# A two-layer attention and expert kernel: first loads in pieces, key reload issued from two queues, last round reordered

## What is computed

```
x = x + attention1(norm(x), ctx)          # 16 heads of 8, softmax over all 1601 context rows
x = x + experts1(norm(x))                 # 9 experts of 352, two chosen per token, sigmoid gate
x = x + attention2(norm(x), ctx, idx)     # 64 context rows per token, named by idx (all below 256)
x = x + experts2(norm(x))                 # 8 experts of 176, two chosen, softmax gate, and a shared one
experts:  sum_e  cw[t, e] * (silu(x w1[e]) * (x w3[e])) w2[e]
attention2: the rows in idx count as often as they are named (a count per token and context row)
```

## Time and profile before

| | us |
|---|---|
| median of 3 runs | 1551.48 (1540.69 to 1551.87) |
| the profiled execution's own time | 1554.78 |
| its span | 1553.0 |
| PE busy | 1381.9 |
| DVE busy | 1105.1 |

### The profile page before, as it was taken

The page is one execution under the profiler, slowest core; times in us unless marked ns, Lnnn a source line. Parts: engine busy times, 40 slices in busy tenths (PEclk is TensorE's granted clock), DMA queues, the critical chain, the costliest instruction groups (busy, mean ns, idle before and its releaser), DMA issues.

```text
span 1553.0 us, 34000 instructions
## 1 busy us (share of the span) xinstructions
PE 1381.9 (89%) x12530; PEld 805.4 (52%) x12588; DVE 1105.1 (71%) x2284; ACT 776.7 (50%) x1191; POOL 825.1 (53%) x1379
## 2 busy tenths in 40 slices
PE   4499899999998899989988999989999899889966
PEld 3143474347743476435843476435754467335835
DVE  4586468877688567986598767886688776895353
ACT  3155525762376524764266723765257633665242
POOL 4146345664457445665457554675456744553542
PEclk9698899999999999999999999999999999999977
DMA  3704330023201431024300331013200231002201
GB/s 87 164 12 127 80 78 1 22 75 85 55 8 30 85 75 41 12 50 94 82 1 32 66 92 46 12 40 104 66 18 22 68 80 42 2 2 57 56 1 45
DMA packets 97622, 82.12 MB, mean 53 GB/s; under 512 B 17626, under 2 KB 90612, under 8 KB 97460
## 3 DMA queue, kind: packets, MB, share of 16 engines
q1 hardware_dynamic: 97460, 79.95, 20.9%
HBM read 67.29 MB, written 12.61 MB: 51 GB/s over the span
## 4 chain that ended last, share of the span: by engine, by line
PE 61%; DVE 20%; issue 6%; POOL 6%; ACT 4%; DMA 2%; SPq 1%; POOLq 0%; DVEq 0%; ACTq 0%
PE ob L763 11%; PE ob L837 8%; DVE mx L1216 7%; PE um L821 7%; PE um L822 6%; PE um L748 6%; PE um L733 5%; PE um L711 3%; DVE big L1327 2%; DVE mx L1331 2%; DVE xn L1115 2%; PE um L883 2%; DVE big L1260 2%; PE um L686 1%; PE um L705 1%
## 5 line engine op out<-in xcount | busy, mean ns | idle before, releaser
L1216 DVE TENSOR_REDUCE mx<-um 128x2 f32<-128x802 f32 (+1 forms) x512 | 501.0, 988 | 173.5 <-PE um L733 169.9
L1021 ACT ACTIVATE probs<-um 128x1024 f32<-128x1024 f32 (+1 forms) x448 | 425.7, 962 | 210.2 <-PE um L748 205.7
L1406 POOL TENSOR_TENSOR hid<-hid,cwb 128x256 f32<-128x256 f32 (+1 forms) x304 | 216.9, 730 | 279.2 <-DVE hid L1228 134.6
L1027 ACT ACTIVATE hid<-um 128x256 f32<-128x256 f32 (+1 forms) x304 | 116.8, 384 | 357.2 <-PE um L822 357.1
L1412 POOL TENSOR_TENSOR big<-iotab,idx_lo 128x512 bf16<-128x512 bf16 x256 | 272.5, 1079 | 30.8 <-PE um L923 23.0
L763 PE MATMUL ob<-probs,vaug 128*9 128x256 f32 (+1 forms) x3328 | 280.6, 386 | 2.6 <-ACT oT L1003 2.0
L733 PE MATMUL um<-kst,qa 64*128 64x401 bf16 (+1 forms) x1024 | 178.4, 347 | 29.7 <-DVE mx L1216 16.6
L748 PE MATMUL um<-big,kst 64*128 64x256 bf16 (+1 forms) x1664 | 171.0, 279 | 10.1 <-DVE mx L1216 3.9
L1228 DVE TENSOR_TENSOR hid<-hid,um 128x256 f32<-128x256 f32 (+1 forms) x304 | 124.7, 415 | 67.3 <-ACT hid L1027 64.6
L821 PE MATMUL um<-xnT,w1T 128*128 128x256 f32 (+1 forms) x400 | 128.0, 402 | 0.0
L837 PE MATMUL ob<-w2T,hid 128*128 128x128 f32 (+1 forms) x800 | 123.6, 279 | 3.5 <-POOL hid L1406 2.5
(11 more groups left out here) (218 smaller groups left out, 2065.4 us busy)
## 6 DMA issues: line engine op xcount, KB each, us to landing
kst<-k_parts SPq DMA_DIRECT2D x384, 50.0 KB
cwb<-cw_rows SPq DMA_DIRECT2D x112, 128.0 KB, 3.5
k_parts<-big SPq DMA_DIRECT2D x72, 128.0 KB, 1.9
ctx_sb<-in_ctx SPq DMA_DIRECT2D x8, 768.0 KB
cwb<-cw_rows SPq DMA_DIRECT2D x48, 96.0 KB, 3.0
k1st<-k_parts SPq DMA_DIRECT2D x96, 32.0 KB
cwb<-cw_rows SPq DMA_DIRECT2D x48, 64.0 KB, 2.7
cwb<-cw_rows SPq DMA_DIRECT2D x16, 112.0 KB, 3.1
```

The lines of the kernel that those rows point to most:

```text
L1021: act.activation(probs[0:kn, k:k + 2, 0:w], own_banks, ACT.Exp).then_inc(f_read, 1)
L1216: dve.tensor_reduce(mx[:, p % 2, s, :, j], pair[:, :, 0:w], AX, ALU.max, negate=True).then_inc(u_read, 1)
L1406: pool.tensor_tensor(h, h, cwb[0:nr, k, :], ALU.mult).then_inc(hw_ready, 1)
```

## The change

Loads: the context of batch 0 comes in four pieces with a semaphore each (`ctx0_in`), with `Wkv` and the key bias between them (`wkv_in`), then `x`; `Wo`, `bv`, `Wq`, `bqs`, `bo` (`wa_in`, now five) and the indices last; the gate bias goes with the square weights. PE waits for one piece per `ctx`, and for `wa_in` in a new event `pre`, at -46.9. ACT first copies two values (its table load comes with it). The memset of `kst` is split between POOL (pairs 0, 1) and DVE, that of `k1st` goes to POOL behind `idx`. Reload of batch 0: SP issues the half `hh = 0`, ACT the other. `x`, indices and context of batch 1 are issued at -31.95, between `rel` 0 and `rel` 1. `all0` of batch 0 stands behind `ctx` 3. Expert weights are transposed from 23.127 on (before 14.886), `w2T` from 42.939 (45.331).

Last round: the pairs of batch 6's attention 2 start at `XL - 6.339 = 49.66` of round 7, 3.0 apart; its layer norm and gate chain 24.258 before `XL`'s place (so `nm1` at 78.94, `ct1` at 88.13); its layer-2 chunks at `R + 0.422`, 0.489 apart, in front of and among the lone attention 2 of batch 7. The reload of `k1st` is an event `rel1` of its own; for batch 7 it comes at 81.33, `kv1` at 85.56 and `mq` at 86.08. Layer-1 chunks of batch 7 no longer wait in the order for layer 2 of batch 6. `SHIFT` moves 19 named events by 0.02 to 0.73 units in all batches.

```diff
-'pairl': 1.461, 'c1': 6.259, 'b_all0': -41.0, 'b_w1': 14.886, 'b_w2': 45.331, 'b_w2s': 1.6
+'pairl': 1.336, 'c1': 6.247, 'b_all0': -37.556, 'b_w1': 23.127, 'b_w2': 42.939, 'b_w2s': 1.387
+'b_pre': -46.9, 'b_ldc1': -31.95, 'z_rel1': 25.333, 'z_kv1': 29.559, 'z_mq': 30.079, 'z_pair0': -6.339, 'z_pair': 3.0, 'z_back': -24.258, 'z_chunk': 0.422, 'z_each': 0.489
+SHIFT = {('cnt', 11): -0.621, ('part', 44): 0.293, ('mu', 2): -0.526, ('eq', 14): 0.727, ('c0', 6): 0.325, ...}
-                at.append((t, len(at), kind, b, n))
+                at.append((t + SHIFT.get((kind, n), 0.0), len(at), kind, b, n))
-                put(prep + AT["ldx"], "ldx", b)
-                put(prep + AT["ldc"], "ldc", b)
+                put(prep + AT["ldx"] if b >= 2 else AT["b_ldc1"], "ldx", b)
+                put(prep + AT["ldc"] if b >= 2 else AT["b_ldc1"], "ldc", b)
...
+                put(own + (AT["kk1"] + 0.01 if b < NB - 1 else XL + AT["z_rel1"]), "rel1", b)
+                put(own + (AT["kv1"] if b < NB - 1 else XL + AT["z_kv1"]), "kv1", b)
...
+                first, back, chunk, each = chain + AT["pair0"], chain, chain + Y1, C1
+                if b == NB - 2:
+                    step, first, back = AT["z_pair"], chain + XL + AT["z_pair0"], chain + XL + AT["z_back"]
+                    chunk, each = chain + R + AT["z_chunk"], AT["z_each"]
...
-            sp.dma_start(wkv_sb[:, :], Wkv).then_inc(wa_in, 16)
+            load_ctx0(0)
+            sp.dma_start(wkv_sb[:, :], Wkv).then_inc(wkv_in, 16)
+            load_ctx0(1)
+            sp.dma_start(bk_col[:, :], bkv[0:D].rearrange("(p a) -> p a", a=1)).then_inc(wkv_in, 16)
+            load_ctx0(2)
+            sp.dma_start(xs[0][:, :, :], x[0:1].rearrange("a (s p) d -> p (a s) d", p=P)).then_inc(x_in, 16)
+            load_ctx0(3)
...
-                        for hh in range(2):
+                        for hh in range(1 if b == 0 else 2):
                             r = SLOT * hh + HD * term
                             sp.dma_start(kst[r:r + HD, 2 * n:2 * n + 2, 0:NK], src[hh, :, 2 * n:2 * n + 2, :]).then_inc(kst_in[n], 16)
...
+                elif kind == "rel" and b == 0:
+                    if n == 0:
+                        act.wait_ge(key0_out, 16 * 3 * 4)
...
+                    for term in range(NT):
+                        src = k_parts[0, KPART[term]].rearrange("(a h d) k -> h d a k", h=2, d=HD)
+                        r = SLOT + HD * term
+                        act.dma_start(kst[r:r + HD, 2 * n:2 * n + 2, 0:NK], src[1, :, 2 * n:2 * n + 2, :]).then_inc(kst_in[n], 16)
...
+            copy(veps[:, :, :], neg_half[:, :, :]).then_inc(act_warm, 1)
...
+            dve.memset(kst[:, 2:NP, :].rearrange("p a k -> p (a k)").bitcast(f32), TWO_ONES).then_inc(kst_half, 1)
...
+            pool.memset(kst[:, 0:2, :].rearrange("p a k -> p (a k)").bitcast(f32), TWO_ONES).then_inc(kst_one, 1)
```

More of the change, by code:

```diff
@@ L67, in rows @@
+SHIFT = {('cnt', 11): -0.621, ('part', 44): 0.293, ('part', 45): 0.198, ('part', 26): -0.337, ('cnt', 14): -0.483, ('df', 28): -0.156, ('df', 7): 0.309, ('df', 8): 0.309, ('w1', 1): -0.211, ('pair1', 7): 0.319, ('part', 3): -0.1, ('part', 57): -0.306, ('key', 3): -0.019, ('cnt', 12): -0.118, ('mu', 2): -0.526, ('dk', 25): -0.13, ('eq', 6): -0.334, ('eq', 14): 0.727, ('c0', 6): 0.325}
 def rows(c, total):
@@ L360, in order_rest @@
                 put(own + AT["kk1"], "key", b, 4)
-                put(own + AT["kv1"], "kv1", b)
+                put(own + (AT["kk1"] + 0.01 if b < NB - 1 else XL + AT["z_rel1"]), "rel1", b)
+                put(own + (AT["kv1"] if b < NB - 1 else XL + AT["z_kv1"]), "kv1", b)
                 for kind in ("nm0", "aT0", "o0", "n1", "n1a", "xT1", "gate0", "le0", "rt0", "msk", "mq"):
-                    put(own + XL + AT[kind], kind, b)
+                    put(own + XL + (AT["z_mq"] if kind == "mq" and b == NB - 1 else AT[kind]), kind, b)
                 put(own + XL + AT["ct0"], "ct0", b)
@@ L428, in build @@
         EV = order()
+        for kind, b in {ev[:2] for ev in EV}:
+            own = [ev[2] for ev in EV if ev[:2] == (kind, b) and (kind != "part" or ev[2] % PARTS == PARTS - 1)]
+            assert own == sorted(own) or kind in ("sta", "std", "cl")
         turn, users, loads = {}, {}, {}
@@ L523, in _, with load_ctx0 @@
         def _(sp):
+            def load_ctx0(n):
+                c0, c1 = 4 * n, min(4 * n + 4, KC - 1)
+                if n < 3:
+                    sp.dma_start(ctx_sb[:, c0:c1, :], ctx_in[0:1, c0 * P:c1 * P, :].rearrange("a (c p) d -> p (a c) d", p=P)).then_inc(ctx0_in[n], 16)
+                else:
+                    sp.dma_start(ctx_sb[0:KLAST, KC - 1, :], ctx_in[0:1, (KC - 1) * P:NK, :].rearrange("a k d -> (a k) d")).then_inc(ctx0_in[n], 16)
             def load_ctx(b):
@@ L841, in _ @@
             pe.wait_ge(const_ready, 2)
-            pe.wait_ge(wa_in, 16 * 8)
-            pe.wait_ge(pre_bv, 1)
-            pe.matmul(quarter[1][:, 0:D], xn[:, 0, :], wo_sb[:, :], start=True, stop=True).then_inc(pre_psum, 1)
-            pe.wait_ge(pre_bo, 1)
             for ev in EV:
                 kind, b, n = ev
-                if kind == "part":
+                if kind == "pre":
+                    pe.wait_ge(wa_in, 16 * 5)
+                    pe.wait_ge(pre_bv, 1)
+                    pe.matmul(acc[:, 0:D], xn[:, 0, :], wo_sb[:, :], start=True, stop=True).then_inc(pre_psum, 1)
+                elif kind == "part":
                     max_part(b, n)
```

128 lines of the change are left out of this document (72 added, 56 removed).

## The result

The changed kernel takes 1533.62 us (median of 20 runs, 1527.51 to 1544.09) against 1548.82 in the runs beside it: ratio 0.9916, interval 0.9897 to 0.9936, some 13 us faster (15 by the medians). The forecast was 1527, 24.5 us faster, in a range from 1506 to 1544. Its profiled execution took 1533.95 (span 1531.8). That of before took 1554.78, 6 us over its median, so the two profiles lie 21 us apart and part of that is not the change.

A forecast was written before the change was run, and what follows sets the result against it. PE, busy 89%, was taken as the bound, with gains only where it is idle or slow. Start -16, last round -8.5 and shifts 0 gave -24.5 us: 1527 on the median of 1551.48, range 1506 to 1544.

The forecast's parts named there:

- Start: Batch 0's loads and reload: first maximum 6.2 us earlier, batch 1's hole 9.5 us shorter; -15.7 us together, bounds -9 and -21.
- not what ends last: First pair's reload of 12 DMAs: transfers, not the 4.2 us of issuing, end last, so a second queue gains 0.
- The hole: PE's 9.44 us idle before batch 1's context transposes, waiting for the context load behind 48 reload DMAs; forecast to go, -9.5 us.
- rival (a): The hole before batch 1's transposes stays; only -6 to -8 us of the start comes, 1536 us; chance 0.14.
- Last round: Batch 6's attention 2 and layer-2 chunks moved around batch 7: -23 + 10 + 4.5 = -8.5 us, bounds -16 and +2.
- Stage 1: Batch 7's attention 1, which batch 6's attention 2 mostly leaves: -23 us, bounds -26 and +3.
- rival (c): Batch 7's attention 1 does not shorten when attention 2 leaves it: +3 instead of -23, 1553 us; chance 0.05.
- From the last combine to the layer-1 sum: Batch 7's gate chain and first experts: +8 from round 0's length, 2 for table loads; +10 us, bounds +6 and +20.
- The lone attention: Batch 7's attention 2 behind batch 6's chunks: first pair +5.5, pairs gain 1; +4.5 us, bounds 0 and +8.
- check against conservation: Last round: 17 us of work moves into the lone attention's hole, which can fill at most 17; about half comes out.
- Shifts: 19 events of each batch move by under one group: 0 us, bounds -5 and +5.
- Rival (b): Lone attention's pairs run at full clock and chunks vanish in idle PE, or second queue doubles reload: 1519 us; chance 0.19.

The follow-up runs named there:

- e4: Changed kernel with its last round put back as before and the table of small shifts emptied, leaving only the new start; 1535.37 us, ratio to before 0.9912.
- e3: Changed kernel with all 24 reload transfers of batch 0 issued by SP, none by ScalarE's queue; 1535.05 us, ratio to before 0.9922.
- e2: Changed kernel with only the table of small shifts emptied; 1531.00 us, ratio to before 0.9896.
- e5: Changed kernel plus fillers (unused 128x512 matmuls) ahead of waits in batch 7's first gate chain and four pairs of batch 6; ratio to before 0.9899.
- e8: Changed kernel with fillers in batch 7's first gate chain and batch 6's pairs, also in the last four lone pairs and last gate chain; 1526.76 us, ratio 0.9882.
- e12: Changed kernel with fillers in both last gate chains and pairs, and also at the start (reload wait, first 16 max parts); 1529.16 us, ratio to before 0.9857.
- e7: Changed kernel with its last round put back, plus four tiny Exp among batch 7's first experts, adding eight table loads; ratio to before 0.9912.
- e6: Changed kernel with the pairs of batch 6's attention 2 placed 2.0 units apart from -8.5 instead of 3.0 from -6.3; ratio to before 0.9899.
- e9: Changed kernel with batch 6's pairs tight (2.0 apart from -8.5) and fillers in both gate chains and the last lone pairs; ratio to before 0.9876.
- e11: Changed kernel with batch 6's 13 layer-2 chunks beside batch 7's lone pairs (8.0 units later, 1.0 apart) instead of ahead; ratio to before 0.9971.

## Why the prediction was right in its time and wrong in a step

**Start.** Forecast -15.7, measured -15.6 in the pair of profiles (12.8 to 16.7 over all of them); e4 alone is 12 us faster by medians. The index cast ended at 10.96 (forecast 11.4), ctx 3 came at 20.35 (20), POOL's last low part ended at 25.1 (24) and VectorE's at 25.5, the first maximum came at 37.10 (37). Within it two terms were off and cancelled, which is luck: the reload started 1.8 us late (29.5, not 27.7), and the first pair, for which the forecast kept 9.3 us, took 7.6. What was wrong here is that issuing is "not what ends last": 12 issues took 4.0 us before and 2.45 with two queues, and the first maximum followed the last of them by 5.2 and 5.1 us. That issue outran transfer over all 48 did not make it free for the first 12. The hole went as forecast (9.44 to 0), which settles rival (a).

The Trainium skill (DMA: Bandwidth & Descriptors, "Issuing engines are not separate DMA queues") says that all queues end on the same engines and that a second issuing engine saves only the time of issuing, usually small beside the transfer. The gain of nothing was the forecast's reading of it, not the page's. Of the 2.8 us between e3 and the changed kernel 2.1 are such time, which agrees with the page; what the other 0.7 is was not tried.

**Last round.** This is the failed step: -8.5 forecast, about -1 measured. Single profiles of one order differ by 3 to 5 us, so the terms are taken from the means of the four old and the three new rounds of the table without fillers:
- Stage 1: -23 forecast, -21.5 measured. Right but for 1.5, and rival (c) fell.
- From the last combine to the layer-1 sum: +10 forecast, +12.6 measured, 1.7 in the gate chain and 10.9 in the experts. The forecast took the length from round 0 (60.7 us, and 2 for table loads), and the three new rounds take 65.0 in the mean. Of the 2.3 us more than 62.7, 1.7 have a cause that no term named. The last product of layer 1 ends at 1447.0, and VectorE begins the sum 1.8 us later. Batch 6's second routing and the copy of `maskq` stand in front of it in its queue; that is read from the timeline, and no run moved them:

```profile
1446.35 0.66 PE L863 MATMUL ob<-w2T,hid 96*128 96x128 f32 x4
...
1448.45 0.42 DVE L1361 COPY maskq<-um 128x512 bf16<-128x512 bf16 x1 [0.17 <-DVE cw L1201]
1448.79 0.41 DVE L1274 TENSOR_TENSOR x<-ob,x 128x256 f32<-128x256 f32 x1
```

  It is 1.8 us in e2 and e3 too, and under 0.1 before and in round 0. The half clock behind the last combine is not a miss against the analog, since round 0 had it as well over its gate chain:

```profile
181.40:196.00 14.60, 9.49 (x35) 5.42 (x34) 11.30 (x35) 1.24 (x3) 4.73 (x6) 0.56 0.23 48
```

  Against the kernel before, whose chain ran at 1.00 under layer 2's chunks, the half clock is the 1.7 of the chain: 16.5 us in the mean of three, 14.7 with the fillers of e5, e8 and e12. The 2 us charged for table loads have no support (0 in e7, and in e6 the stage fell only by PE's own work), which leaves that much more of the stretch without a cause. PE is busy 59.5, 60.0 and 56.2 us in it against the 53.1 of round 0, more than the "nearly as much" of the forecast.
- The lone attention: +4.5 forecast, +7.5 measured. Its first pair is right: +5.5 forecast, 18.5 us after the sum against 13.0. Its pairs are the largest miss: they were to gain 1 from full clock, and took 31.3 us (30.1 to 32.3) instead of 29.3 (27.5 to 31.1), +2. The clock did rise with the chunks in front, from 0.67 to 0.81 in the old rounds to 0.84 to 0.88, and the pairs did not get shorter for it. A table load of 1.28 before their first Exp and the down products left among them are new there; which weighs how much was not tried.
- The end: 0 forecast, +0.2 measured.

So 3.0 us of the 7.3 missed are the pairs, 2.6 the stretch of the gate chain and the experts, 1.5 stage 1. The forecast's check against conservation (17 us of work into the hole, half comes out) was the wrong account. The chunks had been filling another gap, the gate chain's, and moving them opened it: over the whole round PE's idle time fell by 6.4 us, and 6.6 came back as busy time, part of it at half clock.

**Shifts.** 0 forecast, 0 within what can be measured (e2: 1531.00, interval 0.9867 to 0.9924).

**What would show it.** Right: the first maximum at 37.10, no wait on `ctx_sb`, no new wait on the keys, 12 table loads in the last 240 us, attention 1 of batch 7 at 1.53 us a group (85.9 / 56), the first lone pair 18.5 us behind the sum. Wrong: the first pair of keys took 7.6 us and not still 9; the clock between the last two attentions, forecast above 0.9, was 0.59 in its first 17 us. The total lies inside the range because the range took in a last round of +2; of the forecast's 24.5 us only 13 to 15 came. That the two profiles lie 21 us apart, near the 24.5, is luck of the clock: 6 us of it are the stretch from 67 to 384 us of the kernel before at 0.95.

**Rival (b)** asked for more from the pairs or a doubled rate from the queue. The queue brought 1.7 of the 3.6 us of its bound, the pairs nothing.

## What to carry to other kernels

Dense work moved into one gap leaves the gap that it filled before: price the place it comes from as closely as the place it goes to, and compare the idle time of the whole round. Look at the granted clock in windows of a few us over every new thin stretch. A few filler products ahead of a wait gave 1.2 to 2.6 us in each of two gate chains (the last stage took 29.1 or 29.2 us in four profiles with them, 30.5 to 31.7 in ten without); in the lone attention no gain could be shown. Two functions of ScalarE's tables alternated at no cost where ScalarE was busy 20 of 37.5 us, and at a high one where the loads filled it. Where a burst of small transfers is awaited, count the issues ahead of the last one: halving 4.5 us of them was worth about 2. And before a difference of 1 or 2 us is given to an edit, look for it in other profiles that lack the edit: the late first maximum of e2 was in e7 and e9 as well.

## What the runs showed of the hardware

- From the first reload issue to the first maximum matmul, 11 profiles with two issuing queues moved 127 to 154 GB/s, those with one 110 (e3) and 82 (before). Most of the time saved is issuing: 12 transfers took 4.5 us to issue from one queue and 2.45 from two.
- The round of batch 2 took 176.9 us at a granted clock of 1.00 and that of batch 1 183.4 at 0.96, in one execution and with the same work. Whole executions of the changed kernel follow the clock too: 1527.5 and 1529.5 us at 0.972, 1544.1 at 0.960.
- Four of 12 profiles with a ScalarE queue had PE at half clock from 24 to 28 us (0.50, the others 0.79 to 1.00), and in them the first reload issue of ScalarE came at 30.3 to 30.5 us instead of 28.5 to 29.5 (30.7 in e12, where SP's was as late).
- A table load showed 1.28 us each time; eight of them cost 0 beside the experts (e7), and with sixteen among the pairs of e11 ScalarE was busy 31.5 of 32 us.
